# Small SBUF tiles and a 192-byte gap allocated ahead of the large ones in a four-layer graph network kernel

## The kernel before

| tiles | begins at | past a multiple of 512 |
|---|---|---|
| raw, B | 1,152 | 128 |
| xs1, xs0, nat0, nat1, rrep, ring, glo / ring_g, identf | 132,224 to 203,904 | 128 |
| r16 | 204,416 | 128 |
| sml, epst, bad, worst, flag | 204,480 to 205,600 | 192, 192, 224, 256, 288 |
| bias, W1, Tw / stg0, stg1, embn / W | 205,632 to 223,552 | 320 |
| ring_x | 224,832 | 64 |

## Time and profile before

### The profile page before, as it was taken

How to read it: one execution, slowest core, us unless ns; L and a number is a source line. 1 busy time by engine, 2 the same in 40 slices (tenths; PEclk the granted TensorE clock), 3 DMA queues, 4 the chain that set the end, 5 groups by cost and what they waited for, 6 DMA issues and landing times.

```text
span 1286.5 us, 16492 instructions
## 1 busy us (share of the span) xinstructions
PE 1259.8 (98%) x6048; PEld 1046.0 (81%) x6048; DVE 731.1 (57%) x1819; ACT 241.3 (19%) x436; POOL 62.0 (5%) x52
## 2 busy tenths in 40 slices
PE   7999999999999999999999999999999999999996
PEld 6888878778878787878888888888888888888875
DVE  5836897787776777788724543451246245334424
ACT  5622111121112101110112122121112121121211
POOL 0000000000000000000001001000000010010000
PEclk9999999999999999999999999999999999999998
DMA  9722112211112111110000000010001000000000
GB/s 339 315 98 59 37 51 60 70 52 39 45 51 60 40 37 37 30 50 13 15 1 1 1 1 1 1 66 1 1 25 42 1 1 1 1 1 1 33 1 35
DMA packets 28517, 55.08 MB, mean 43 GB/s; under 512 B 3584, under 2 KB 14336, under 8 KB 26368
## 3 DMA queue, kind: packets, MB, share of 16 engines
q1 hardware_dynamic: 28432, 53.96, 12.8%
HBM read 41.89 MB, written 12.06 MB: 42 GB/s over the span
## 4 chain that ended last, share of the span: by engine, by line
PE 91%; DVE 5%; DMA 1%; issue 1%; ACT 1%; SPq 1%; DVEq 0%; ACTq 0%
PE ps L606 29%; PE ps L607 29%; PE ps L715 20%; PE ps L624 7%; PE ps L618 2%; PE ps L645 2%; PE ps L646 2%; DVE nat L972 1%; DVE ring L972 1%; DMA raw<-in_at 1%; DVE xs L882 1%; ACT xs L749 0%; SPq L1012 0%; DVE sml L914 0%; DVE sml L905 0%
## 5 line engine op out<-in xcount | busy, mean ns | idle before, releaser
L606 PE MATMUL ps<-B,xs 128*128 128x512 f32 x1664 | 658.1, 395 | 3.7 <-DVE xs L882 3.7
L607 PE MATMUL ps<-B,xs 128*128 128x512 f32 x1664 | 649.9, 391 | 0.0
L606 PEld LDWEIGHTS ps<-B,xs 128*128 128x128 f32 x1664 | 312.7, 188 | 68.5 <-ACT xs L749 3.5
L607 PEld LDWEIGHTS ps<-B,xs 128*128 128x128 f32 x1664 | 312.7, 188 | 64.0
L715 PE MATMUL ps<-Tw,xs 128*128 128x512 f32 x1280 | 316.6, 396 | 2.1 <-DVE ring L972 2.1
L715 PEld LDWEIGHTS ps<-Tw,xs 128*128 128x128 f32 x1280 | 238.1, 187 | 61.3 <-DVE ring L972 4.2
L870 DVE TENSOR_TENSOR ring<-ps,rrep 128x512 f32<-128x512 f32 x94 | 64.5, 689 | 278.0 <-PE ps L607 268.0
L972 DVE SCALAR_TENSOR_TENSOR nat<-ps,embn,nat 128x128 f32<-128x128 f32 x448 | 154.0, 344 | 56.1 <-PE ps L715 56.0
L972 DVE SCALAR_TENSOR_TENSOR ring<-ps,embn,ring 128x128 f32<-128x128 f32 x512 | 175.6, 343 | 0.0
L624 PEld LDWEIGHTS ps<-W,ring 128*128 128x128 f32 x896 | 110.4, 191 | 7.9 <-DVE ring L870 3.5
L624 PE MATMUL ps<-W,ring 128*128 128x128 f32 x896 | 113.2, 275 | 2.3 <-DVE ring L870 2.3
(11 more groups left out here) (65 smaller groups left out, 627.0 us busy)
## 6 DMA issues: line engine op xcount, KB each, us to landing
raw<-in_at SPq DMA_DIRECT2D x13, 1024.0 KB, 16.6
ring<-in_xn SPq DMA_DIRECT2D x16, 256.0 KB, 3.0
ring_x<-in_xt SPq DMA_DIRECT2D x32, 128.0 KB, 3.3
ring_x<-y1d SPq DMA_DIRECT2D x32, 128.0 KB, 3.5
out<-nat SPq DMA_DIRECT2D x16, 256.0 KB, 2.4
y1d<-ring SPq DMA_DIRECT2D x14, 256.0 KB, 2.8
zd<-nat SPq DMA_DIRECT2D x12, 256.0 KB, 3.0
nat<-zd SPq DMA_DIRECT2D x3, 1024.0 KB, 5.5
```

The lines of the kernel that those rows point to most:

```text
L606: pe.matmul(bank, x[:, 0, m, :], of, start=m == 0, stop=False)
L607: mm = pe.matmul(bank, x[:, 1, m, :], of, start=False, stop=ends and m == NT - 1)
```

## The change

Six small tiles are allocated first, and behind them a tile "gap" of 48 words (192 bytes) that nothing reads or writes. They fill 64 + 4 x 32 + 512 + 192 = 896 bytes, so that raw and B begin at byte 2,048. Behind identf only sml is left of the small ones; W1, Tw, stg, embn and W begin 192 bytes later than before, at multiples of 512, and ring_x begins 256 past one. No instruction, wait, DMA or shape is changed.

```diff
@@ -319,6 +319,14 @@
         def sem(name):
             return ctx.enter_context(nc.semaphore("s_" + name))
 
+
+        r16s = sb("r16", [P, NT], F32)
+        epst = sb("epst", [P, 1], F32)
+        bad = sb("bad", [P, 1], F32)
+        worst = sb("worst", [1, 1], F32)
+        flag = sb("flag", [1, 1], I32)
+        bias_t = sb("bias", [P, 2, C], F32)
+        sb("gap", [P, 48], F32)
         with ExitStack() as scope:
             raw = sb("raw", [P, NT, N], F32, scope)
         B = sb("B", [P, NT, N], F32R)
@@ -330,13 +338,7 @@
             glo = sb("glo", [P, 512], F32R, scope)
         ring_g = sb("ring_g", [P, 512], F32)
         identf = sb("identf", [P, P], F32)
-        r16s = sb("r16", [P, NT], F32)
         sml = sb("sml", [P, 2, NC, 4, 8], F32)
-        epst = sb("epst", [P, 1], F32)
-        bad = sb("bad", [P, 1], F32)
-        worst = sb("worst", [1, 1], F32)
-        flag = sb("flag", [1, 1], I32)
-        bias_t = sb("bias", [P, 2, C], F32)
         W1 = sb("W1", [P, 2, P], F32)
         with ExitStack() as scope:
             junk = sb("junk", [P, 2, N], BF16, scope)
```

## The result

The changed kernel takes 1278.2 us, the median of four runs (1277.01 to 1279.64), against 1286.25 for the kernel before beside it. The ratio is 0.9936, with a 95% interval of 0.9919 to 0.9953. It is faster by 8 us, 0.6%, where 63 us were forecast. The reason that this rival gave, Tw's own start, did not hold, as the experiments show.

What follows compares the result with a forecast made beforehand. TensorE's matmul count times start-to-start pace was taken as the bound. Terms summed to 67.3 us, less 4 for VectorE left 63 off the 1286.44 median: 1223.5 us, own range 1208 to 1246, 8-in-10 range 1208 to 1288.

Steps and rivals of the forecast that it cites:

- this rival: Only Tw's and W's start is the trouble, B's is not: 12.3 us saved, time 1274, chance 0.27.
- the bound from below is 0.2133, I take 0.2153: Matmuls with B in the passes: pace falls from 0.2268 to 0.2153 us, just above 512 columns at 2.4 GHz.
- this law: Moving operand's bytes to the next multiple of 256, in four-byte words, equal the surplus cycles: 32 for B, 48 for Tw.
- the half-clock stretch: Head, 3 us at 1.2 GHz: B takes 0.4267 us, its columns alone; surplus read as hidden there, a cost of supply.
- 38.3 for B: B in the passes: 3,328 matmuls each 11.5 ns faster, 38.3 us saved.
- 2.0 for the head: 256 B matmuls in the head would save 2.9 us; 2.0 taken because the last adjacency tile waits on DMA.
- Tw's term: 1,280 Tw matmuls falling from 0.2335 to 0.2153 us: 23.3 us saved, ends 25.8, 8.6 or 0.
- The slow intervals behind Tw: Eight B matmuls after a Tw group take 1.81 us instead of 1.83, about 92 times: 1.5 us saved.
- 2.2 us: 896 passes with W or W1, each 2.4 ns faster: 2.2 us saved, ends 0 and 4.
- What VectorE takes back: Deduction for VectorE becoming late: 2 us from 160 to 215 us, 2 us for growing waits from 215 to 620.
- The slower rival: All starts at one residue collide, B rises to 0.2335 us: 24 us lost, time 1310, chance 0.13.
- The rival of no effect: Start addresses do not matter; Tw differs by load order and PSUM banks: time 1286.4, chance 0.19.

Runs made afterwards that it cites:

- paces: Separate kernel computing nothing of the reference, timing groups of 48 matmuls at chosen starts: float32r 512 columns 0.227 us at both +64, float32 passes 0.112, transposes 0.108.

## Why the prediction was wrong

The reading of the bound, the paces and the counts stood. The list of what the change touches stood too: VectorE's subtraction takes 685 ns from nat and 686 from stg, against 686 and 686 in the earlier trace rows, and B's and W's passes are unchanged.

**The step that failed is "the bound from below is 0.2133, I take 0.2153"** and the argument that carried it: that B's 32 and Tw's 48 surplus cycles are both the way from the start to the next multiple of 256 bytes. The changed kernel has B at a multiple of 512, where this law leaves no surplus, and B still takes 0.2268. That the law, with no free size, fitted two points was a coincidence. The 13.4 ns of B stay at a start of 0, 64, 128 and 192 alike as long as the load begins with it. They are there with float32r at 256, 320 and 384 columns too, and bfloat16 has 2.7 ns instead. From the half-clock stretch the prediction went to a cost of supply, and from there to the address; the stretch only shows that the cost is not one of array cycles. Of the 67.3 us, 38.3 for B and 2.0 for the head were thus never there.

**Tw's term** was right in kind and too large: 23.3 us were taken, 8.6 was written beside it as the end "down to B's pace", and that is what happened: summed from start to start, the 1,246 Tw matmuls that another follows at once lost 7.7 us. Its cause, though, is not Tw's own start, which the rival named as off a multiple of 128: Tw at 64 past a multiple of 512 is as fast as at 0 when xs is at 64 too. The rival had the right remark in passing, that load and moving operand of B begin at the same residue and those of Tw do not.

**The slow intervals behind Tw** went as written: 1.83 to 1.81 us for eight, 1.9 us over all B matmuls of the T stage (the forecast had 1.5). **W's** 2.2 us did not come: its passes stay at 0.111, and float32 passes at aligned starts in paces have 0.112 beside transposes with 0.108, so the difference is one of the operation.

**What VectorE takes back** was put at 4 us of 67. Here it is PE's idle time in the T stage, 499.40 - 494.50 = 4.9 us before and 491.20 - 485.25 = 5.95 after: 1.05 us. Summed from start to start, Tw's intervals lost 7.7 us and B's 1.9, and the 38 intervals of 0.3 us and more, which hold waits, grew by 1.35; together that is the 8.2 us of the stage. Behind it PE waits as before, and VectorE's accumulation still sets only the few waits at the change of a pair.

**The slower rival**, equal starts that collide, is refuted in the strongest form: equal starts are the fastest of the table. B at 0.2333 is real, but for the opposite layout, B 64 bytes before xs (1299 us). **The rival of no effect** fell with the kernel in which Tw was moved: only addresses differ, and Tw's pace with them.

**The range.** 1278.2 lies outside the forecast's own 1208 to 1246 and inside the wide 1208 to 1288. The wide range had been drawn over the rivals' cases, so that the hit says nothing for the mechanism of the forecast.

**The two rules cited.** By the Trainium skill (TensorE: Matmul & The Clock Gate, Back-to-back issue gap) a warm matmul of 512 columns takes 216 ns. The page says this of an isolated matmul, which the prediction left out, and gives about 131 ns for a stream of them. The stream of bfloat16 matmuls here has the 216 ns, 10.37 us for 48, and not 131; float32r has neither, at 0.2267 at its best. The Trainium skill (SBUF — State Buffer, the note on cachelines) has cachelines of 16 bytes; that starts at multiples of 16 make no difference was the prediction's inference from it. The T stage moved by 8.2 us with all starts multiples of 32, so the inference fails.

**Open.** Why a difference of 64 costs 2 ns and one of 192 costs 6.6, which of the loads has to agree, and what the 13.4 ns are. The runs exclude that they are proportional to the moved columns, and at 512 moved columns to the loaded ones.

## What to carry to other kernels

Let the moving operand of a float32r matmul with 512 columns and its load begin at the same place modulo 256 bytes, both at multiples of 32; here one gap of 64 bytes in front of Tw does all that the change does, and aligning both to 512 does no more. When two rates in a trace fit a neat law, look for what else the pair has in common before the law is carried to a third point: B and Tw differed both in their own start and in their start relative to xs. A kernel of groups of 48 equal matmuls, each group with its own line, prices such a thing in one short run.

## What the runs showed that was not expected

- The pace of float32r matmuls of 512 columns, at starts that are multiples of 64, depends on the difference of the two starts in SBUF modulo 256 bytes, with a sign: 0.2267 to 0.2273 us at 0, 0.229 at +64 (0.2333 in two groups at +320), 0.2319 to 0.2333 at 128, 0.2329 to 0.2335 at +192. bfloat16 (0.216) and float32 passes of 128 columns (0.112) showed no such dependence at the one difference tried, 64 bytes either way.
- At 256 moving columns the order turns round: 0.120 at equal starts (139.14 - 133.39 over 48), 0.118 with the moving operand at +64 or +192.
- Fewer loaded columns make a 512-column float32r matmul slower at equal starts, 0.2300 at 64 columns against 0.2267 at 128, and a 256-column one faster, 0.1138 against 0.120.
